# Token stages: the second copies of q's high part for head group 0 issued by ACT instead of SP

## The chip, the cores and the metric

The kernel runs on one core of one Trainium2 chip. The metric is the device time of the whole program in microseconds (us); lower is better. The engines are named as in the profile: PE is TensorE's matmuls and PEld its weight loads, DVE is VectorE, ACT is ScalarE, POOL is GpSimd, SP is SyncE, whose work here is to issue DMAs. An engine's name with a q behind it (SPq, ACTq) stands for what its sequencer does itself: DMA issues, semaphore waits, register work.

## What is computed

A transformer stack of two layers on 8192 tokens of width 512. The part that matters here is the cross attention that stands in both layers, ahead of a mixture of experts in the first layer and a light and heavy feed-forward in the second:

```python
q = split_heads(layernorm(x) @ Wq.T + bq)            # 16 heads of 32
k, v = split_heads(ctx @ Wk.T + bk), split_heads(ctx @ Wv.T + bv)   # 154 keys
scores = (q @ k.T) * tau + delta                      # then over sqrt(32)
x = x + softmax(scores) @ v  (heads joined) @ Wo.T + bo
```

## The kernel before, in words

`token_phase` is called once for each layer (l = 0 and l = 1). Its 8192 tokens are 16 groups of 512, and one turn of its loop works on one group; beside it, in the same turn, stand the end of the group before and the start of the group after. A turn has 16 steps (`st`), each a unit of 128 tokens and 4 heads; steps 0 to 3 are head group 0, steps 4 to 7 head group 1, and so on. The names in a turn i: `cur` is the group whose scores are computed, `nxt` the one after it, `prev` and `prev2` those before. The order of instructions on every engine is written out by hand, and engines meet through semaphores only. SP, POOL, DVE and PE run 12 of the turns in a hardware loop; ACT is unrolled.

The products of q and k are computed to full precision in one matmul per head: the rows of the moving side `kst` are k's high part, k's high part again and k's low part (32 rows each, then two rows for delta), and the stationary side `stack` holds under them q's high part, q's low part and q's high part again, and ones. So each head of q's high part is copied into `stack` twice, at rows 0 and 64, and its low part once, at row 32. These are copies from SBUF to SBUF between partitions, and they go by DMA: for each head group 4 heads, thus 8 copies of q's high part (L344) and 4 of its low part (L348), 64 KB each. SP issues all of them, in `stack_up`.

The chain for head group 0 of the next group of tokens, whose q is made ahead of its turn: PE's `query` (steps 10 and 11, L785) gives it, ACT adds the bias (`query_out`, L612, step 12), DVE rounds it to q's high part (`query_high`, L69, step 12), POOL subtracts to get q's low part (`query_low`, L407, step 12), SP copies both into `stack`, and PE's `scores` at step 0 of the next turn (L722) waits until `stacked0` has counted all 12 copies:

```python
if t == 0:
    pe.wait_ge(s[f"kv_in{g}"], 48 * i + 48)
    pe.wait_ge(s[f"stacked{g}"], STACK * i + STACK)
```

In each step ACT computes four exponentials (L691, each with a read of its sum behind it), which wait for DVE's `negmax` (L471) of the same unit. In layer 1, ACT also scales the finished tokens in steps 12 to 14 (`scaled`, L654). DVE copies transposed probabilities (L494) and normalises the finished group (L460) in steps 0 and 1. POOL scales the probabilities (L414). On SP, what follows `stack_up(i + 1, 0)` in a turn is, in layer 1, the store of z (L375, which waits for ACT's last `scaled`), then the store of xs (L378, which waits for DVE's `residual` of step 14), and the load of `xbo` (L381), each 1 MB.

Of the kernel before, what the change touches and what calls it, by code (L numbers as in the profile page):

```python
# [12 lines left out]
F32 = mybir.dt.float32  # L13
# [12 lines left out]
HEADS, DK = 16, 32  # L26
HG = P // DK
GROUPS = HEADS // HG
TROWS = HG * KTAIL
DC = D // P  # L30
# [208 lines left out]
def reached(engine, sem, value):  # L239

    if not (isinstance(value, int) and value <= 0):
        engine.wait_ge(sem, value)


def token_phase(nc, l, a, scr, c, x_in, x_rows):
    gate = l == 0
    with ExitStack() as ctx:
        def sb(name, shape, dt=F32):
            return ctx.enter_context(nc.sbuf_tensor(f"t{l}_{name}", shape, dt))
# [8 lines left out]
        qhigh, qlow = (sb(f"q_{part}", [P, 2, D], F32R) for part in ("high", "low"))  # L258
        qT = sb("qT", [P, 2, D])
        stack = sb("stack", [KROWS, HEADS, D], F32R)  # L260
# [13 lines left out]
        else:  # L274
# [4 lines left out]
        s = Sems(nc, ctx, f"t{l}",  # L279
                 "w_in wq_in kv_in0 kv_in1 kv_in2 kv_in3 x_in xbo_in ready ones x_stored z_stored "  # L280
                 "stacked0 stacked1 stacked2 stacked3 x_stats x_mv x_ve x_rstd xn xbo xnT_mm xnT_dve xnT_act "
                 "q_mm q_out q_high q_low scored negmax exped inv normed p_mm pTm pTt pv oT_out proj resid "
                 "s_stats s_mv s_ve s_rstd xl z z_mm zT_dve zT_act side_mm side_out top "
                 "ssq ssq_c rn score dot part_mm part logit")
# [39 lines left out]
        @block.sync  # L324
        def _(sp):
            sp.dma_start(x[:], rows(x_in, 0)).then_inc(s["x_in"], 16)
            sp.dma_start(wq[:], a[f"WqT{l}"].rearrange("(k p) n -> p k n", p=P)).then_inc(s["wq_in"], 16)
            with nc.allow_non_contiguous_dma(reason="biases by partition"):
                sp.dma_start(bq[:], a[f"bq{l}"].rearrange("(k p) -> p k", p=P)).then_inc(s["w_in"], 16)
            sp.dma_start(bo[:], a[f"bo{l}"].partition_broadcast(P)).then_inc(s["w_in"], 16)  # L330
            for g in range(GROUPS):
                load_kv(sp, 0, g)
            sp.dma_start(wo[:], a[f"WoT{l}"].rearrange("(k p) n -> p k n", p=P)).then_inc(s["w_in"], 16)
            if gate:
                sp.dma_start(wg[:], a["gateT"].rearrange("(k p) n -> p k n", p=P)).then_inc(s["w_in"], 16)
            else:
                sp.dma_start(rt[:], a["routing"].partition_broadcast(P)).then_inc(s["w_in"], 16)

            def stack_up(j, n):

                sp.wait_ge(s["q_high"], DC * j + n + 1)
                for at in (0, 2 * DK):
                    for h in range(HG):
                        sp.dma_start(stack[at:at + DK, HG * n + h, :].bitcast(F32),  # L344
                                     qhigh[h * DK:(h + 1) * DK, n % 2, :].bitcast(F32)).then_inc(s[f"stacked{n}"], 16)
                sp.wait_ge(s["q_low"], DC * j + n + 1)
                for h in range(HG):
                    sp.dma_start(stack[DK:2 * DK, HG * n + h, :].bitcast(F32),  # L348
                                 qlow[h * DK:(h + 1) * DK, n % 2, :].bitcast(F32)).then_inc(s[f"stacked{n}"], 16)

            def turn(i, par, prev2, prev, cur, nxt, nxt2):
                if cur:
                    stack_up(i, 1)
                if prev2 and gate:
                    sp.wait_ge(s["z"], TG * (i - 1))
                    sp.dma_start(rows(scr["xw"], i - 2, D), z[:]).then_inc(s["z_stored"], 16)
                if cur:
                    stack_up(i, 2)
                if prev and cur:
                    load_kv(sp, i, 2, GROUPS * i - 1)  # L360
                    load_kv(sp, i, 3, GROUPS * i)
                if nxt2:
                    reached(sp, s["xn"], TG * (i + 2))
                    sp.dma_start(x[:], rows(x_in, i + 2)).then_inc(s["x_in"], 16)
                if cur:
                    stack_up(i, 3)
                if cur and nxt:
                    load_kv(sp, i + 1, 0, GROUPS * i + 1)
                    load_kv(sp, i + 1, 1, GROUPS * i + 2)
                if nxt:  # L370
                    stack_up(i + 1, 0)
                if prev2 and not gate:
                    sp.wait_ge(s["z"], TG * (i - 1))
                    sp.wait_ge(s["score"], i - 1)
                    sp.dma_start(rows(scr["xs"], i - 2), z[:]).then_inc(s["z_stored"], 16)  # L375
                if prev:
                    sp.wait_ge(s["resid"], TG * i)
                    sp.dma_start(rows(x_rows, i - 1), xs[:]).then_inc(s["x_stored"], 16)  # L378
                if cur:
                    reached(sp, s["resid"], TG * i)  # L380
                    sp.dma_start(xbo[:], rows(x_in, i)).then_inc(s["xbo_in"], 16)  # L381

            turns(sp, turn)
            sp.wait_ge(s["z_stored"], 16 * NG)
            sp.wait_ge(s["x_stored"], 16 * NG)
# [220 lines left out]
        def _(act):  # L606
# [30 lines left out]
            def part_out(j):  # L637
                act.wait_ge(s["part_mm"], j + 1)
                reached(act, s["side_mm"], j)
                act.copy(part[:], ps[:, B_BANK, :]).then_inc(s["part"], 1)  # L640

            def square(j, t):
                act.wait_ge(s["xl"], TG * j + t + 1)
                if t == 0:
                    reached(act, s["rn"], j)
                else:
                    act.wait_ge(s["ssq"], TG * j + t)
                act.activation(junk2[:], z[:, t, 0:D], ACT.Square,
                               accum_out=ssq[:, t:t + 1]).then_inc(s["ssq"], 1)

            def scaled(j, tiles):
                act.wait_ge(s["rn"], j + 1)
                for t in tiles:
                    act.mul(z[:, t, 0:D], z[:, t, 0:D], rn[:, t:t + 1]).then_inc(s["z"], 1)  # L654

            def turn(i, par, prev2, prev, cur, nxt, nxt2):
                j = i - 2
                for st in range(UNITS):
                    if cur and st == 2:
                        query_out(i, 2)  # L660
                    if st == 2 and prev:
                        o_out(i - 1, 1 - par, 2)
                        p_tail_out(i - 1, GROUPS - 1)
                    if st in (6, 10, 14) and cur:
                        p_tail_out(i, st // TG - 1)
                    if cur and st == 4:
                        query_out(i, 3)
                    if st == 4 and prev:
                        o_out(i - 1, 1 - par, 3)
                    if st in (8, 12) and cur:  # L670
                        o_out(i, par, st // TG - 2)
                    if nxt and st == 12:
                        if not cur:
                            act.wait_ge(s["w_in"], W_IN)
                        query_out(i + 1, 0)
                    if cur and st == 0:
                        query_out(i, 1)
                    if gate and prev2 and st in (4, 12):
                        z_turned(j, Z_AT[st])
                    if nxt and st in (8, 10):  # L680
                        x_turned(i + 1, X_AT[st])
                    if not gate and prev2 and st in (3, 5, 7, 9):
                        square(j, (st - 3) // 2)
                    if cur:
                        u = st
                        act.wait_ge(s["negmax"], UNITS * i + u + 1)

                        reached(act, s["p_mm"], UNITS * i + u - 3)
                        for h in range(HG):
                            at = (h % 2) * KEYS  # L690
                            op = act.activation(pr[:, u % 4, :, h], ps[:, 2 * (u % 2) + h // 2, at:at + KEYS], ACT.Exp,  # L691
                                                bias=negmax[:, u, h:h + 1], accum_out=total[:, u, h:h + 1])
                        op.then_inc(s["exped"], 1)
                    if gate and prev2 and st == 13:
                        part_out(j)
                    if not gate and prev2 and st in (12, 13, 14):
                        if st == 12:
                            act.wait_ge(s["dot"], TG * (i - 1))
                        scaled(j, {12: (0,), 13: (1, 2), 14: (3,)}[st])

            unrolled(turn)

# [1324 lines left out]
```

## Time and profile before

| | |
|---|---|
| median of 3 runs | 4095.25 us (4093.11 to 4096.59) |
| the profiled execution | 4095.83 us, its span 4093.3 us |
| PE busy over the span | 3568.4 us, 87% |
| DVE, POOL, ACT busy | 67%, 47%, 36% |
| mean granted TensorE clock | 0.929 of full speed |
| L344, copies of q's high part | 1024 issues of 64 KB by SP |
| L348, copies of q's low part | 512 issues of 64 KB by SP |

The time stands 2.5 us above the span in the profiled execution; a change of the span is taken as the same change of the time. DMA issues are not counted as busy time. Times of rows are microseconds from the start of the span.

### The profile page before, as it was taken

To read this page: it belongs to the slowest core of one execution; us is meant where nothing else is said; L and a number is where in the kernel's file an instruction comes from. 1 tells how busy PE (TensorE), PEld (TensorE's weight loads), DVE (VectorE), ACT (ScalarE), POOL (GpSimd) and SP (SyncE) were. 2 spreads that over 40 slices of the span, in tenths; PEclk is the share of its full clock that TensorE was granted. 3 is DMA by queue.
4 is the path that set the end of the run, shared out by engine and by line. 5 is a ranking of instruction groups with operands and counts; after the bars stand their busy time and mean duration, and the time that the engine had idled before them with its cause. 6 is when DMAs were issued, how large, how long until landed. Compare 5 with 4: busy or idle time off the path is not lost. (4 is left out here: it accounts for less than half of the span.)

```text
span 4093.3 us, 56822 instructions
## 1 busy us (share of the span) xinstructions
PE 3568.4 (87%) x16277; PEld 2413.9 (59%) x16277; DVE 2724.6 (67%) x5471; ACT 1492.1 (36%) x5333; POOL 1918.5 (47%) x1784
## 2 busy tenths in 40 slices
PE   8599999999837999999996999999999696249998
PEld 4355555555426777777774555555555475227776
DVE  3477777777687677677673677777776443366665
ACT  0365666666400111111111666666666221201110
POOL 0255555555401777767773556555555232012332
PEclk9799999999955999999997999999999898569999
DMA  5455545454312666666664456555653555000111
GB/s 159 129 147 151 144 141 166 143 143 138 110 42 69 169 165 161 163 170 159 161 168 105 126 137 169 147 152 138 166 153 113 188 216 208 12 21 6 20 21 18
DMA packets 323211, 523.11 MB, mean 128 GB/s; under 512 B 59257, under 2 KB 104121, under 8 KB 322553
## 3 DMA queue, kind: packets, MB, share of 16 engines
q1 hardware_dynamic: 290808, 443.79, 36.6%
q0 software_dynamic: 32256, 77.65, 10.1%
q8 instruction: 58, 0.95, 0.1%
q14 instruction: 89, 0.72, 0.1%
HBM read 283.64 MB, written 136.96 MB: 103 GB/s over the span
## 5 line engine op out<-in xcount | busy, mean ns | idle before, releaser
L691 ACT ACTIVATE t_pr<-ps,t_negmax 128x154 f32<-128x154 f32 x2048 | 867.9, 547 | 529.4 <-DVE t_negmax L471 528.7
L414 POOL TENSOR_TENSOR t_pr<-t_pr,t_inv 128x616 f32<-128x616 f32 x512 | 642.6, 1256 | 616.3 <-DVE t_inv L486 613.6
L494 DVE COPY t_pTm<-ps 128x512 f32<-128x512 f32 x512 | 349.9, 683 | 315.0 <-PE ps L735 310.7
L785 PE MATMUL ps<-t_xnT,t_wq 128*128 128x512 f32 x1024 | 505.2, 617 | 19.1 <-ACT t_qT L612 18.9
L806 PE MATMUL ps<-t_wo,t_oT 128*128 128x512 f32 x1024 | 497.9, 610 | 7.8 <-DVE t_xs L503 6.6
L734 PEld LDWEIGHTS ps<-ident,t_pr 128*128 128x128 f32 x2048 | 317.9, 204 | 296.1 <-issue 258.0
L691 ACT ACTIVATION_READ_ACCUMULATOR t_pr<-ps,t_negmax 128x1 f32 x2048 | 472.1, 230 | 0.0
L471 DVE TENSOR_REDUCE t_negmax<-ps 128x4 f32<-128x616 f32 x512 | 403.1, 787 | 30.1 <-PE ps L722 29.6
L734 PE MATMUL ps<-ident,t_pr 128*128 128x128 f32 x2048 | 334.4, 286 | 51.7 <-DVE t_pTm L494 36.1
L722 PE MATMUL ps<-t_kst,t_stack 98*128 98x154 f32 x2048 | 340.1, 289 | 15.0 <-DMA t_stack<-t_q_low 13.2
L785 PEld LDWEIGHTS ps<-t_xnT,t_wq 128*128 128x128 f32 x1024 | 176.9, 192 | 229.4 <-issue 203.2
L74 PE MATMUL ps<-e_xT_high,e_wgu_high 128*128 128x512 f32 x768 | 307.2, 400 | 1.6 <-DVE e_xT_low L1248 1.6
L76 PE MATMUL ps<-e_xT_high,e_wgu_low 128*128 128x512 f32 x768 | 305.2, 397 | 0.0
L75 PE MATMUL ps<-e_xT_low,e_wgu_high 128*128 128x512 f32 x768 | 303.3, 395 | 0.0
L806 PEld LDWEIGHTS ps<-t_wo,t_oT 128*128 128x128 f32 x1024 | 176.0, 191 | 185.9 <-issue 166.4
L722 PEld LDWEIGHTS ps<-t_kst,t_stack 98*128 98x128 f32 x2048 | 272.7, 194 | 21.8 <-issue 19.5
L1208 POOL DMA_INDIRECT x_dram<-e_y,e_put_idx x128 | 246.1, 1923 | 30.8 <-issue 30.5
L407 POOL TENSOR_TENSOR t_q_low<-t_qT,t_q_high 128x512 fp32r<-128x512 f32 x128 | 174.0, 1359 | 167.9 <-DVE t_q_high L69 167.9
L1316 ACT ACTIVATE e_sig<-ps 128x512 f32<-128x512 f32 x96 | 57.5, 599 | 527.1 <-PE ps L76 527.1
L1288 DVE TENSOR_TENSOR e_h<-e_sig,ps 128x512 f32<-128x512 f32 x96 | 65.7, 685 | 245.9 <-ACT e_sig L1316 245.8
L1798 POOL TENSOR_TENSOR h_w_low<-c_hw,h_w_high 128x512 fp32r<-128x512 f32 x64 | 89.7, 1404 | 248.0 <-DVE h_w_high L69 248.0
L439 POOL TENSOR_TENSOR t_xbo<-t_xbo,t_bo 128x512 f32<-128x512 f32 x128 | 166.7, 1304 | 64.7 <-DMA t_xbo<-x_dram 64.0
(291 smaller groups left out, 7342.8 us busy)
## 6 DMA issues: line engine op xcount, KB each, us to landing
t_stack<-t_q_high SPq DMA_DIRECT2D x1024, 64.0 KB, 2.2
e_wgu_in<-in_gate_upT SPq DMA_DIRECT2D x32, 1536.0 KB, 6.5
t_stack<-t_q_low SPq DMA_DIRECT2D x512, 64.0 KB, 2.0
x_dram<-t_xs SPq DMA_DIRECT2D x32, 1024.0 KB, 5.7
t_kst<-kst_dram SPq DMA_DIRECT2D x128, 235.8 KB
e_wd_in<-in_downT SPq DMA_DIRECT2D x32, 768.0 KB
xs_dram<-t_z SPq DMA_DIRECT2D x16, 1032.0 KB
l_z<-xs_dram SPq DMA_DIRECT2D x16, 1032.0 KB
```

Source lines behind the costliest of these rows:

```text
L74: pe.matmul(out, left[0], right[0], start=start, stop=False)
L75: pe.matmul(out, left[0], right[1], start=False, stop=False)
L76: return pe.matmul(out, left[1], right[0], start=False, stop=stop)
L414: pool.tensor_tensor(p, p, inv[:, v, :].unsqueeze(1).to_broadcast([P, KEYS, HG]), ALU.mult).then_inc(s["normed"], 1)
L471: dve.tensor_reduce(negmax[:, u, :].rearrange("p (b h) -> p b h", b=2), ps[:, q:q + 2, 0:2 * KEYS].rearrange("p b (h n) -> p b h n", h=2), ...
L494: dve.tensor_copy(pTm[:, g % 2, :, t * P:(t + 1) * P], ps[:, 4, :].rearrange("p (h n) -> p h n", h=HG)).then_inc(s["pTm"], 1)
L691: op = act.activation(pr[:, u % 4, :, h], ps[:, 2 * (u % 2) + h // 2, at:at + KEYS], ACT.Exp, bias=negmax[:, u, h:h + 1], accum_out=total[ ...
L722: mm = pe.matmul(ps[:, 2 * (u % 2) + h // 2, at:at + KEYS], stack[:, HG * g + h, t * P:(t + 1) * P], kst[:, g, h * KEYS:(h + 1) * KEYS], s ...
L734: pe.transpose(ps[:, 4, h * P:(h + 1) * P], pr[:, v % 4, 0:P, h], ident[:])
L785: mm = pe.matmul(ps[:, A_BANK, :], wq[:, k, n * P:(n + 1) * P], xnT[:, k, :], start=(k == 0), stop=(k == DC - 1))
L806: mm = pe.matmul(ps[:, A_BANK, :], oT[:, par, k, t * P:(t + 1) * P], wo[:, k, :], start=(k == 0), stop=(k == DC - 1))
L1208: pool.indirect_dma_start(out=scr["x1"][:, :], out_offset=bass.IndirectOffsetOnAxis(ap=put_idx[:, n:n + 1], axis=0), in_=y[q][:, n, :], in ...
```

## The change

For head group 0 alone, SP no longer issues the four second copies of q's high part (to rows 64 to 95 of `stack`). ACT issues them, behind its exponentials of step 14 (in layer 1 behind `scaled` of that step too), after a wait for `q_high`. The count that PE waits for is the same 12 copies. Head groups 1 to 3 are left as they were.

```diff
             def stack_up(j, n):
 
                 sp.wait_ge(s["q_high"], DC * j + n + 1)
-                for at in (0, 2 * DK):
+                for at in (0, 2 * DK) if n else (0,):
                     for h in range(HG):
                         sp.dma_start(stack[at:at + DK, HG * n + h, :].bitcast(F32),
                                      qhigh[h * DK:(h + 1) * DK, n % 2, :].bitcast(F32)).then_inc(s[f"stacked{n}"], 16)
...
+            def stack_again(j):
+                act.wait_ge(s["q_high"], DC * j + 1)
+                for h in range(HG):
+                    act.dma_start(stack[2 * DK:3 * DK, h, :].bitcast(F32),
+                                  qhigh[h * DK:(h + 1) * DK, 0, :].bitcast(F32)).then_inc(s["stacked0"], 16)
+
...
                         scaled(j, {12: (0,), 13: (1, 2), 14: (3,)}[st])
+                    if nxt and st == 14:
+                        stack_again(i + 1)
```

On ACT, before, in steps 13 to 15 of a turn of layer 1 and the first of the next (the exponentials are L691, `scaled` is L654, `query_out` L612):

```order
L654 ACTIVATE t_z<-t_z,t_rn 128x512 x2
L624 COPY t_pTt<-ps 104x512
L691 ACTIVATE t_pr,t_total<-ps,t_negmax 128x154 x4
L654 ACTIVATE t_z<-t_z,t_rn 128x512
L691 ACTIVATE t_pr,t_total<-ps,t_negmax 128x154 x4
L612 ACTIVATE t_qT<-ps,t_bq 128x512
L691 ACTIVATE t_pr,t_total<-ps,t_negmax 128x154 x8
```

The same place in the change, where the lines behind the insertion have other numbers:

```order
L660 ACTIVATE t_z<-t_z,t_rn 128x512 x2
L624 COPY t_pTt<-ps 104x512
L697 ACTIVATE t_pr,t_total<-ps,t_negmax 128x154 x4
L660 ACTIVATE t_z<-t_z,t_rn 128x512
L645 DMA t_stack<-t_q_high 32x512 x4
L697 ACTIVATE t_pr,t_total<-ps,t_negmax 128x154 x4
L612 ACTIVATE t_qT<-ps,t_bq 128x512
```

Four DMA issues now stand between the exponentials of step 14 and those of step 15; in layer 0 they stand there too, with no `scaled` ahead of them. On SP, at the end of a turn of layer 0:

```order
 L322 DMA t_vt<-vt_dram 104x128
-L344 DMA t_stack<-t_q_high 32x512 x8
+L344 DMA t_stack<-t_q_high 32x512 x4
 L348 DMA t_stack<-t_q_low 32x512 x4
 L378 DMA x_dram<-t_xs 128x4x512
```

Four issues are gone ahead of the copies of q's low part and of what is queued behind them. This is so in each of the 16 turns of a layer that make a next q: once before the first scores, and 15 times between two turns.

## Rows read from the trace of the kernel before

**Rows 1.** Windows of both layers: length; busy PE, PEld, DVE, ACT, POOL; clock, DMA share.

```profile
320.00:1035.00 715.00, 704.08 (x3527) 418.82 (x3526) 536.71 (x1141) 434.95 (x1751) 393.30 (x340) 1.00 0.52 148
2460.00:3090.00 630.00, 601.71 (x2867) 348.95 (x2866) 484.46 (x1035) 422.76 (x1676) 372.93 (x316) 0.99 0.56 151
```

**Rows 2.** Timeline of PE at the end of a turn of layer 0: start, us, what.

```profile
562.26 0.65 PE L722 MATMUL ps<-t_kst,t_stack 98*128 98x154 f32 x4
563.50 1.98 PE L785 MATMUL ps<-t_xnT,t_wq 128*128 128x512 f32 x4 [0.59 <-ACT t_qT L612]
```

**Rows 3.** Timeline of SP at the same place.

```profile
551.41 4.95 SPq L344 DMA_DIRECT2D t_stack<-t_q_high  x8
556.40 2.49 SPq L348 DMA_DIRECT2D t_stack<-t_q_low  x4
559.09 0.43 SPq L378 DMA_DIRECT2D x_dram<-t_xs  x1
559.72 0.41 SPq L381 DMA_DIRECT2D t_xbo<-in_x  x1
```

**Rows 4.** Timeline of ACT at the same place, first exponential of units and query_out.

```profile
558.09 0.55 ACT L691 ACTIVATE t_pr<-ps,t_negmax 128x154 f32<-128x154 f32 x1 [0.86 <-DVE t_negmax L471]
...
559.24 0.54 ACT L691 ACTIVATE t_pr<-ps,t_negmax 128x154 f32<-128x154 f32 x1
...
561.23 0.54 ACT L691 ACTIVATE t_pr<-ps,t_negmax 128x154 f32<-128x154 f32 x1 [1.45 <-DVE t_negmax L471]
```

**Rows 5.** Semaphore waits of ACT's own sequencer, windows 557.5:559 and 2749.9:2750.3.

```profile
L242 ACTq EVENT_SEMAPHORE  x1: 17/17/17, 558.1 to 558.1; - x1
L242 ACTq EVENT_SEMAPHORE  x1: 17/17/17, 2750.1 to 2750.1; - x1
```

**Rows 6.** Timeline of layer 1 at the end of a turn: PE, ACT and SP.

```profile
2754.11 0.65 PE L722 MATMUL ps<-t_kst,t_stack 98*128 98x154 f32 x4
2750.51 0.59 ACT L691 ACTIVATE t_pr<-ps,t_negmax 128x154 f32<-128x154 f32 x1
2752.01 0.78 ACT L654 ACTIVATE t_z<-t_z,t_rn 128x512 f32<-128x512 f32 x1
2753.08 0.54 ACT L691 ACTIVATE t_pr<-ps,t_negmax 128x154 f32<-128x154 f32 x1 [0.28 <-DVE t_negmax L471]
2749.92 2.49 SPq L348 DMA_DIRECT2D t_stack<-t_q_low  x4
2752.99 0.43 SPq L375 DMA_DIRECT2D xs_dram<-t_z  x1
```

**Rows 7.** L348 and L344 by source in 551:559 and 526:533: issue ns, landing.

```profile
L348 SPq DMA_DIRECT2D t_stack<-t_q_low x4: 590/590/591, 556.4 to 558.3; - x4
DMA to landing us min/median/max: 2.0/2.0/2.2
L344 SPq DMA_DIRECT2D t_stack<-t_q_high x8: 527/590/1532, 526.9 to 532.3; - x8
DMA to landing us min/median/max: 3.1/3.9/5.8
```

**Rows 8.** Gathers on POOL's queue behind a 768 KB load of SP's, 1530:1536.

```profile
L1194 POOL DMA_INDIRECT e_xe<-xw_dram,e_idx x4: 946/955/1037, 1531.2 to 1535.0; - x4
DMA to landing us min/median/max: 3.4/4.1/4.8
```

**Rows 9.** Timeline of DVE at the end of the turn of rows 2.

```profile
556.06 0.69 DVE L503 TENSOR_TENSOR t_xs<-ps,t_xbo 128x512 f32<-128x512 f32 x1 [1.84 <-PE ps L806]
...
563.26 0.78 DVE L471 TENSOR_REDUCE t_negmax<-ps 128x4 f32<-128x616 f32 x1
```

**Rows 10.** Timeline of PE where scores of step 0 waited for copies.

```profile
158.83 1.11 PE L722 MATMUL ps<-t_kst,t_stack 98*128 98x154 f32 x4 [5.85 <-DMA t_stack<-t_q_low]
210.51 0.65 PE L722 MATMUL ps<-t_kst,t_stack 98*128 98x154 f32 x4 [1.20 <-issue]
266.74 0.67 PE L722 MATMUL ps<-t_kst,t_stack 98*128 98x154 f32 x4 [0.59 <-DMA t_stack<-t_q_low]
```

## The prediction

> **What bounds the kernel now.** The windows come first: in layer 0 from 320 to 1035 us, PE is busy for 704.08 of 715 us at full clock, and in layer 1 for 601.71 of 630 us [rows 1]. PE is the bound of the token stages, so a change counts only if it moves PE. Then the timelines of the five engines at one turn boundary of each layer. In layer 0 the scores of step 0 start at 562.26, directly behind PE's own work, with no idle time shown ahead of them [rows 2]; SP's last copy of q's low part is issued by 558.89 (556.40 + 2.49) [rows 3], and such a copy lands 2.0 to 2.2 us after its issue begins [rows 7]. The last of the four begins at 558.3, so everything is there by 560.5, 1.8 us before PE wants it. In layer 1 the scores start at 2754.11; the last low copy begins at 2749.92 + 3 x 0.62 = 2751.78 and lands at 2753.8 to 2754.0, 0.1 to 0.3 us ahead [rows 6, 7]. So before the change the copies are just in time, and SP's issue time is the price of PE only where a row says so: before the first scores (5.85 us of waiting at 158.83 in layer 0, and one like it in layer 1) and at three of the 30 boundaries: 1.20 us, 0.59 us and, of the same kind as the latter, 0.94 us in layer 1 [rows 10].
>
> **What the change takes from SP.** Four issues of 0.62 us each, 2.5 us (4.95 us for eight [rows 3]), leave SP ahead of q's low copies. At an ordinary boundary nobody waits for SP there, so this is worth nothing on PE. Ahead of the first scores of each layer the whole chain waits for SP: 2.5 us each, 5.0 us together. At the three boundaries of [rows 10] at most the idle time shown: 1.2 + 0.6 + 0.9 us; I take 2.5 us, since at the first of them ACT's `query_out` is the next limit. Gain: 7.5 us.
>
> **What the change gives to ACT.** The disputed point is when ACT issues. Counted naively, the four issues start when the exponentials of step 14 are through. The rows say otherwise. Each unit of exponentials has a semaphore wait of the sequencer's own ahead of it (for PE's transposes). The one that belongs to step 15 is executed at 558.1, as the first exponential of step 14 starts (558.09), and not after its last (559.24) [rows 4, 5]. So ACT's sequencer walks past instructions whose waits are met while the engine still works them off; a DMA issue is sequencer work and stands in just this place of the order. In layer 1 the wait of step 15 is executed at 2750.1, before even the first exponential of step 14 starts (2750.51) and though `scaled` (2752.01) lies between [rows 5, 6]. I therefore let the four issues begin at 558.12 in layer 0 and 2750.1 in layer 1, at SP's pitch of 0.62 us, for which ACT has no row of its own.
>
> In layer 0 they end at 560.6. Step 15's exponentials start at 561.23, when DVE's maximum is there [rows 4]: 0.6 us of cover, ACT loses nothing. If the pitch were 0.76 us (eight issues behind a load begin from 526.9 to 532.3, one of them lasting 1532 ns [rows 7]) they would end at 561.2, still free. In layer 1 they end at 2752.6 against 2753.08 [rows 6]: 0.5 us of cover, and 0.1 us lost at the longer pitch. Behind ACT's issues are queued those exponentials and then `query_out` of step 0, for which PE already waits 0.59 us in layer 0 [rows 2]; that is who pays if the cover is gone.
>
> **When the last copy lands.** Layer 1: the last issue begins at 2751.96. SP stores z only at 2752.99, so nothing large is in flight, and the landing is 2.0 to 2.2 us: 2754.0 to 2754.2 against 2754.11. I take +0.05 us for each of the 12 ordinary boundaries, 0.6 us.
>
> Layer 0: the last issue begins at 558.12 + 1.86 = 559.98. But SP, with 2.5 us less to do, has its 1 MB store and 1 MB load out sooner: its low copies end at 556.4, the store waits for DVE's residual, done at 556.75 [rows 9], and goes out about 557, the load about 557.6, instead of 559.09 and 559.72 [rows 3]. ACT's copies, which used to be ahead of these two on SP's queue, now meet them on the DMA engines. The price has no row of its own. From below: 2.0 us, as with idle engines. From above: 5.8 us, the slowest copy issued right behind a 1 MB load on the same queue (the fastest of these took 3.1) [rows 7]. Nearest is a small transfer on another queue beside SP's load: POOL's gathers, where the one with most of the load in flight lands after 4.8 us and the one with least after 3.4 [rows 8]. That is up to 1.4 us for company. I take 1.1 us, a landing of 3.1 us, thus 563.1: the scores of step 0 are 0.85 us late.
>
> The Trainium skill has a rule for this in "DMA: Bandwidth & Descriptors", section "Queues, rings and completion order": a DMA engine takes turns between queues, but a whole packet of one queue at a time. By it a copy on ACT's own queue waits for a packet or so of SP's load and not for all of it, and the 5.8 us of the same queue would be too dear; no run here has shown it yet.
>
> What 0.85 us costs PE: DVE's maximum of step 0 starts at 563.26 with no idle time ahead of it, so DVE is busy until then [rows 9], while the scores are through by 562.91. So 0.35 us of it is hidden on DVE, and of what is left the chain maximum, exponentials, `query_out` of the next step goes on with it. I take 0.4 us at each of 13 ordinary boundaries of layer 0: 5.2 us.
>
> **Sum.** 5.2 + 0.6 - 7.5 = -1.7 us on a profiled time of 4095.83 us, which is 0.6 us above the median of the runs shown. Forecast: 4095 us, no change to speak of. A measurement of this kernel tells about 0.2% (8.2 us) from nothing.
>
> **The rivals.**
>
> *ACT issues late (slower).* The sequencer may not begin a DMA before the engine has worked off what stands ahead. Then the issues run from 559.6 to 562.1 in layer 0 (559.24 + 0.38 of pitch), and step 15's exponentials, `query_out` and PE's L785 are 0.9 us late; the last copy lands at 561.5 + 3.1 = 564.6, 2.3 us late, less 0.35. In layer 1 they run from about 2752.7 to 2755.2, and the last copy lands beside the store of z at 2754.5 + 3.1 = 2757.6, 3.5 us late, of which about 2.8 reach PE. 13 x 1.95 + 12 x 2.8 - 5 = 54: 4150 us. For it: no row shows a DMA issue on ACT. Against it: [rows 5]. It decides from the point where the issues begin after about 558.4.
>
> *The sequencer's lead is shorter (slower, little).* The row at 2750.1 has nine or more instructions not yet done ahead of it. If the DMAs get less of a lead than that wait did, by 0.4 to 0.8 us, layer 1 loses 12 x 0.6 = 7 us: 4102 us.
> The Trainium skill's "Advanced Engine Details and Errata", section "Engine Queue Depths", gives ScalarE a queue of 8, which would set the issues back to where some of the exponentials have run; the row at 2750.1 does not bear this out for a semaphore wait.
>
> *Company on the DMA engines is dear (slower).* If the last copy in layer 0 lands like the copies behind a load on the same queue, after 3.9 to 5.8 us [rows 7], the scores are 1.65 to 3.5 us late, 1.3 to 3.2 after DVE's cover: 13 x that is 17 to 41 us, thus 4106 to 4130 us. For it: both large transfers are out before ACT's first issue. Against it: the queues are two.
>
> *SP's relief is worth all it can be (faster).* No contention, the whole 8 us at the first scores and the three boundaries, and 0.1 to 0.2 us more at each ordinary boundary of layer 1, where the low copies were only just ahead: 4095.8 - 7.7 - 2 = 4086 us. It needs ACT's copies to land in 2.0 us in layer 1 and under 2.6 in layer 0. The same rival stops at -5 or less if two engines that issue at once share what issues, which the first scores would show.
>
> **How the numbers follow.** Forecast 0.50; ACT late 0.10; shorter lead 0.08; dear company 0.20; full relief 0.12. The forecast's own range is 4088 to 4103. The range must leave out no more than 2 in 10: below, 4086, the bound of the full relief; above, 4128, which takes in nearly all of the dear company and leaves out the late ACT. Faster than -0.2% is the full relief: 0.12. Slower by over 0.2% is the late ACT, the dear company and a part of the shorter lead: 0.33. The rest, 0.55, is no change.
>
> **What the profile after would show.** Right: ACTq's four issues begin within 0.1 us of the first exponential of step 14, about 0.6 us apart; step 15's exponentials still wait for DVE; SP's store and load of layer 0 come 2 us sooner; the wait of PE's L722 for a DMA shrinks at the first scores from 5.85 to 3.4 us, and new waits of under 1 us for copies of q's high part appear at the boundaries of layer 0 and none to speak of in layer 1. Wrong: issues after the last exponential, waits of PE above 1.5 us at each boundary, or ACT's issues much longer than 0.6 us.

## The result, and the profile after

| | before | after |
|---|---|---|
| median | 4095.92 us (4093.11 to 4099.02, 4 runs) | 4205.4 us (4202.37 to 4212.62, 4 runs) |
| span of the profiled execution | 4093.3 us | 4210.9 us |
| mean granted TensorE clock | 0.929 | 0.915 |
| PE busy | 3568.4 us | 3613.6 us |

The ratio is 1.027 [1.0252, 1.0287]: the change costs 109 us. The forecast was 4095 us in a range of 4086 to 4128, so the prediction was wrong, and the range too.

Where PE lost the time stands in its costliest groups. On the page of the kernel after, the scores have 96.4 us of idle time ahead of them, 74.3 of it ended by DMAs of q's high part (the same group of before, on its line L722, had 15.0 us of it and was 340.1 us busy, 289 ns a matmul; the query's group had a mean of 617 ns):

```profile
PE 3613.6 (86%) x16277; PEld 2438.6 (58%) x16277; DVE 2731.5 (65%) x5471; ACT 1494.1 (35%) x5333; POOL 1919.8 (46%) x1784
L793 PE MATMUL ps<-t_xnT,t_wq 128*128 128x512 f32 x1024 | 533.5, 647 | 10.5 <-ACT t_qT L612 10.5
L730 PE MATMUL ps<-t_kst,t_stack 98*128 98x154 f32 x2048 | 350.5, 296 | 96.4 <-DMA t_stack<-t_q_high 74.3
```

Waiting grew by 96.4 - 15.0 = 81.4 us and PE's busy time by 45.2 us, together 126.6 us; against it stand shorter waits for other engines (8.6 us of them the query's wait for ACT, 10.5 for 19.1), and the span grew by 117.6 us. By stages, counted from PE's first matmuls in each, the token stage of layer 0 grew by 101.2 us (1037.8 to 1139.0) and that of layer 1 by 14.4 us (992.4 to 1006.8). The 3.5 us in what follows layer 1's token stage (882.2 to 885.7) are not of this change: that part takes 884 to 887 us in the traces of all seven experiments below too. Two things are therefore to be explained: the waits, and why the same matmuls took longer (the query's 647 ns for 617).

The view of waits of PE by releaser, three rows for layer 0 (150 to 1160 us) and then two for layer 1 (2280 to 3300 us); columns are the total, how many, and the longest:

```profile
PE ps L730 <- DMA t_stack<-t_q_high: 64.4, 12, 6.1
PE ps L730 <- issue: 12.4, 3, 5.8
PE ps L730 <- DMA t_stack<-t_q_low: 3.3, 1, 3.3
...
PE ps L730 <- DMA t_stack<-t_q_high: 9.9, 2, 6.1
PE ps L730 <- DMA t_stack<-t_q_low: 3.3, 1, 3.3
```

In layer 0 the scores of step 0 wait at every boundary, 2.2 us at the first and 4.2 to 6.1 us at the others. The three waits put down to "issue" are at the same place of a turn. In layer 1 it is three boundaries of 15 (the two above and one of 3.1 us put down to "issue"); elsewhere nothing. The timeline of PE gives the same in order (start, us, what, and in brackets the idle time before it). Of the 13 scores of step 0 between 320 and 1140 us, the first, one in the middle with the row behind it, and the last:

```profile
338.96 1.13 PE L730 MATMUL ps<-t_kst,t_stack 98*128 98x154 f32 x4 [5.88 <-DMA t_stack<-t_q_high]
...
603.33 1.13 PE L730 MATMUL ps<-t_kst,t_stack 98*128 98x154 f32 x4 [6.05 <-DMA t_stack<-t_q_high]
604.26 3.70 PE L793 MATMUL ps<-t_xnT,t_wq 128*128 128x512 f32 x4
...
1134.69 1.11 PE L730 MATMUL ps<-t_kst,t_stack 98*128 98x154 f32 x4 [5.80 <-issue]
```

Twelve turns take 1134.69 - 338.96 = 795.7 us, 66.3 us each. In the kernel before, the same twelve take 1035.69 - 325.37 = 710.3 us, 59.2 us each:

```profile
325.37 0.65 PE L722 MATMUL ps<-t_kst,t_stack 98*128 98x154 f32 x4
...
1035.69 0.65 PE L722 MATMUL ps<-t_kst,t_stack 98*128 98x154 f32 x4
```

So a boundary of layer 0 costs 7.1 us. From the first scores to those of the last of the 15 boundaries the kernel before needs 876.9 us and this one 979.9 us, 103 us more, nearly the whole result. Not all of the 7.1 us is the wait. The first query matmuls behind the wait take 3.70 us, where those of [rows 2] take 1.98, and the scores themselves 1.13 instead of 0.65. The windows around this boundary say why (length; busy PE, PEld, DVE, ACT, POOL; clock, DMA share):

```profile
596.50:603.30 6.80, 0.78 (x6) 0.49 (x4) 1.57 (x9) 2.00 (x9) 0.85 (x1) 0.91 0.65 189
603.30:607.50 4.20, 4.17 (x8) 2.26 (x9) 3.00 (x5) 1.70 (x8) 2.03 (x2) 0.50 0.06 16
608.50:609.00 0.50, 0.50 (x5) 0.50 (x4) 0.00 (x0) 0.00 (x0) 0.00 (x0) 0.56 0.41 98
609.00:609.50 0.50, 0.50 (x6) 0.50 (x5) 0.43 (x1) 0.00 (x0) 0.00 (x0) 1.00 0.28 70
```

After PE has stood idle for some 6 us, the granted clock is 0.50 (1.2 GHz) until about 608.9, 5.6 us, and then full again. That work would take 2.8 us at full clock. Windows of a quarter of a microsecond behind each of the 15 waits of layer 0 show between 3.3 and 6.6 us at half clock, which costs 1.7 to 3.3 us, 38 us together and 2.5 us in the mean. On the other side PE's wait of 0.59 us for `query_out` [rows 2], which stood at 13 boundaries of layer 0, is gone.

Now the sources of the wait, at the same boundary. SP first, from its copies of q's low part on:

```profile
588.66 2.49 SPq L348 DMA_DIRECT2D t_stack<-t_q_low  x4
591.72 0.43 SPq L378 DMA_DIRECT2D x_dram<-t_xs  x1
592.35 0.41 SPq L381 DMA_DIRECT2D t_xbo<-in_x  x1
```

Then ACT, the exponentials of steps 14 and 15 and its own sequencer's issues among them:

```profile
592.87 0.55 ACT L697 ACTIVATE t_pr<-ps,t_negmax 128x154 f32<-128x154 f32 x1 [0.87 <-DVE t_negmax L471]
592.90 0.52 ACTq L645 DMA_DIRECT2D t_stack<-t_q_high  x1
...
593.45 1.32 ACTq L645 DMA_DIRECT2D t_stack<-t_q_high  x1
...
594.79 1.39 ACTq L645 DMA_DIRECT2D t_stack<-t_q_high  x2
596.29 0.56 ACT L697 ACTIVATE t_pr<-ps,t_negmax 128x154 f32<-128x154 f32 x1 [1.72 <-DVE t_negmax L471]
```

ACT did as forecast: the issues begin 0.03 us after the first exponential of step 14 starts, and the exponentials of step 15 still wait for DVE, as in [rows 4]. ACT's busy time is the same to 2 us, and it is not ACT that is late. But SP's store and load stand ahead of ACT's first issue, by 1.18 and 0.55 us, where before they were issued behind all twelve copies [rows 3]. By source, ACT's copies of this boundary and those of 320 to 1140 us (issue in ns as min/median/max, and from the start of the issue to the landing):

```profile
L645 ACTq DMA_DIRECT2D t_stack<-t_q_high x4: 515/680/1316, 592.9 to 595.6; - x4
DMA to landing us min/median/max: 7.6/7.8/8.2
L645 ACTq DMA_DIRECT2D t_stack<-t_q_high x52: 514/639/1337, 328.7 to 1127.1; - x52
DMA to landing us min/median/max: 5.9/7.5/8.2
```

The last copy begins at 595.6 and cannot be there before 595.6 + 7.6 = 603.2; PE starts at 603.33. What held it is in the DMA queues, for which the windows 592.5 to 598.5, 598.5 to 601.5 and 601.5 to 603.3 us stand here one after the other (packets, MB, share of the 16 engines; q1 is SP's queue, q10 is ACT's):

```profile
q1 hardware_dynamic: 787, 1.58, 93.5%
...
q1 hardware_dynamic: 258, 0.51, 60.7%
q10 hardware_dynamic: 141, 0.20, 29.3%
...
q10 hardware_dynamic: 51, 0.07, 11.0%
q1 hardware_dynamic: 11, 0.01, 2.1%
```

Not a packet of ACT's queue is carried from 592.90 to 598.5, while 1.58 MB of SP's queue are, its store and half of its load; the copies come in as the load runs out. The two large transfers are 2.1 MB, and 787 + 258 + 11 packets of q1 are just these 2.1 MB.

In layer 1 a boundary without this company looks like this in the source view, 2862 to 2872 us, and the scores start at 2869.15 with no wait, since SP issues its stores only from 2868.03 on:

```profile
L645 ACTq DMA_DIRECT2D t_stack<-t_q_high x4: 514/610/613, 2865.1 to 2867.0; - x4
DMA to landing us min/median/max: 2.0/2.0/2.1
```

### The profile page after: what moved, and what is told of

The parts are those of the page before. It is cut to its first block and busy times, and to the rows that moved or that the text cites. A ratio compares the mean times of both kernels' runs of the same rounds, so it can differ in the third digit from the quotient of the medians.

```text
span 4210.9 us, 56822 instructions
## 1 busy us (share of the span) xinstructions
PE 3613.6 (86%) x16277; PEld 2438.6 (58%) x16277; DVE 2731.5 (65%) x5471; ACT 1494.1 (35%) x5333; POOL 1919.8 (46%) x1784
## 5 line engine op out<-in xcount | busy, mean ns | idle before, releaser
L793 PE MATMUL ps<-t_xnT,t_wq 128*128 128x512 f32 x1024 | 533.5, 647 | 10.5 <-ACT t_qT L612 10.5
L730 PE MATMUL ps<-t_kst,t_stack 98*128 98x154 f32 x2048 | 350.5, 296 | 96.4 <-DMA t_stack<-t_q_high 74.3
L742 PE MATMUL ps<-ident,t_pr 128*128 128x128 f32 x2048 | 340.1, 290 | 51.4 <-DVE t_pTm L494 36.6
L730 PEld LDWEIGHTS ps<-t_kst,t_stack 98*128 98x128 f32 x2048 | 282.2, 200 | 105.6 <-issue 105.4
L793 PEld LDWEIGHTS ps<-t_xnT,t_wq 128*128 128x128 f32 x1024 | 186.3, 202 | 227.1 <-issue 212.8
L439 POOL TENSOR_TENSOR t_xbo<-t_xbo,t_bo 128x512 f32<-128x512 f32 x128 | 166.6, 1303 | 59.2 <-DMA t_xbo<-x_dram 58.6
```

The source lines that it names most:

```text
L730: mm = pe.matmul(ps[:, 2 * (u % 2) + h // 2, at:at + KEYS], stack[:, HG * g + h, t * P:(t + 1) * P], kst[:, g, h * KEYS:(h + 1) * KEYS], s ...
L742: pe.transpose(ps[:, 4, h * P:(h + 1) * P], pr[:, v % 4, 0:P, h], ident[:])
L793: mm = pe.matmul(ps[:, A_BANK, :], wq[:, k, n * P:(n + 1) * P], xnT[:, k, :], start=(k == 0), stop=(k == DC - 1))
```

## The experiments

The theory after this reading: ACT's copies are late because SP, relieved of four issues, has its 1 MB store and 1 MB load out ahead of them, and a copy behind them lands only when they have drained, on whichever queue it is. Rivals: copies issued by ACT are slow in themselves, or beside SP's issues; the loss comes from ACT's engine being held up; one of the two transfers alone does it; a queue of its own shelters ACT's copies at least in part. The kernel before, beside which these ran, took 4096.2 us (27 runs) with the first four and 4094.52 us (15 runs) with the last three.

### The store and the load behind the copies

SP waits until all twelve copies have landed before it issues either of the two. ACT still issues the four copies in step 14.

```diff
+                if cur and nxt:
+                    sp.wait_ge(s["stacked0"], STACK * (i + 2))
                 if prev:
                     sp.wait_ge(s["resid"], TG * i)
                     sp.dma_start(rows(x_rows, i - 1), xs[:]).then_inc(s["x_stored"], 16)
```

> The changed kernel, but SP waits until all 12 copies of head group 0 have landed before it issues the store of xs and the load of xbo. Theory (collision): ACT's copies were late by 5 to 6 us in layer 0 because SP's 1 MB store and 1 MB load, issued earlier than before, stood ahead of them on the DMA engines. Then the copies land in 2.0 to 2.2 us again, PE waits for none of them at the ordinary boundaries of layer 0, and the time is 4080 to 4100 us. Rival (ACT's queue): a copy issued by ACT is slow by itself, or is issued too late; then the waits of 5 to 6 us stay, and so does 4190 to 4215 us.

Measured: 4090.85 us (10 runs), ratio 0.9982 [0.9972, 0.9991]; clock 0.929. The whole loss is gone, as the theory had it (4080 to 4100 us). ACT's copies in layer 0, by source:

```profile
L647 ACTq DMA_DIRECT2D t_stack<-t_q_high x50: 514/612/613, 319.7 to 1030.7; - x50
DMA to landing us min/median/max: 2.0/2.0/2.1
```

Issued by ACT at the same place, behind the same exponentials, the copies land in 2.0 us, and PE's waits for them are gone from the view of waits. So neither ACT's issuing nor its place in ACT's program costs anything here; the order against SP's two transfers does. PE's busy time is back at 3569.0 us and the clock at 0.929, so the 45 us of longer matmuls belonged to the waits.

### Only the load behind the copies

The same wait, but behind the store: the store goes out ahead of ACT's copies, the load after them.

```diff
                     sp.dma_start(rows(x_rows, i - 1), xs[:]).then_inc(s["x_stored"], 16)
+                if cur and nxt:
+                    sp.wait_ge(s["stacked0"], STACK * (i + 2))
                 if cur:
```

> The changed kernel, but only the load of xbo waits for the 12 copies; the store of xs goes out ahead of ACT's copies as in the change. Theory (collision): the lateness is the bytes that stand ahead. With 1 MB in place of 2 MB the last copy lands after 4.5 to 5.5 us, the scores of step 0 are 2 to 3 us late at each of about 13 boundaries of layer 0, and the time is 4115 to 4150 us. Rival (only the load from HBM holds copies back, the store does not): as in the run where both wait, 4080 to 4100 us. Rival (any transfer ahead costs the same): 4190 us or more.

Measured: 4097.5 us (10 runs), ratio 1.0005 [0.9996, 1.0015], no difference from the kernel before that can be told, but 6.7 us more than with both transfers behind the copies. The store alone costs much less than I had expected (4115 to 4150 us); the time lies in the range of the rival by which only the load holds copies back. The copies and PE's wait for them (150 to 1180 us):

```profile
L647 ACTq DMA_DIRECT2D t_stack<-t_q_high x52: 514/615/1375, 320.0 to 1034.3; - x52
DMA to landing us min/median/max: 2.0/2.5/3.6
PE ps L732 <- DMA t_stack<-t_q_high: 5.5, 12, 2.2
```

A landing of 2.5 us instead of 2.0, a wait of 0.5 us a boundary. The long issue of 1.3 to 1.4 us, one in four, is still there; it goes with the store in these runs, since it is missing where the load alone is ahead (below).

### ACT's issues two steps earlier

```diff
-                    if nxt and st == 14:
+                    if nxt and st == 12:
                         stack_again(i + 1)
```

> The changed kernel, but ACT issues the four copies behind its exponentials of step 12 instead of step 14, about 6.7 us earlier, and so ahead of SP's store and load. Theory (collision): they land before the large transfers start, no boundary of layer 0 waits, and what SP saves stays: 4080 to 4090 us. ACT's exponentials of step 13 start 0.3 us behind the last issue at the earliest, so up to 0.5 us more at each of 30 boundaries if SP's and ACT's issues slow each other: then 4085 to 4100 us. Rival (ACT's queue is slow by itself): about 8 us of landing would now be hidden too, since the scores come 10 us after the issues, so this run does not speak against it; it tells whether SP and ACT can issue at the same time (both pitches stay 0.62 us) or not (1.2 us).

Measured: 4093.5 us (11 runs), ratio 0.9994 [0.9985, 1.0003], no difference that can be told, and outside the 4080 to 4090 us of the theory. It fits the second range, 4085 to 4100, but not by the condition that stood with it, that SP's and ACT's issues slow each other. In layer 0:

```profile
L645 ACTq DMA_DIRECT2D t_stack<-t_q_high x48: 521/622/866, 370.7 to 1024.1; - x48
DMA to landing us min/median/max: 2.0/2.1/2.4
```

The copies are now issued while SP issues its own eight, and the issue of one takes 622 ns against 612 where ACT issues alone, and one of SP's copies of q's high part 590 ns against 591 in the kernel before (medians): two engines that issue at once do not slow each other. The copies are out before SP's store and load, so the loss is gone without a wait of SP for them. What is gained at the first scores is partly lost in layer 1, where PE waits for ACT's copy of the transposed probabilities 8.7 us in 14 waits (2.9 us in two before). I read this as the four issues standing ahead of that copy on ACT; it was not tried by itself.

### SP issues the same four copies, behind its store and load

ACT issues nothing. This separates the order from the queue.

```diff
-                for at in (0, 2 * DK):
+                for at in (0, 2 * DK) if n else (0,):
...
                     sp.dma_start(xbo[:], rows(x_in, i)).then_inc(s["xbo_in"], 16)
+                if nxt:
+                    for h in range(HG):
+                        sp.dma_start(stack[2 * DK:3 * DK, h, :].bitcast(F32),
+                                     qhigh[h * DK:(h + 1) * DK, 0, :].bitcast(F32)).then_inc(s["stacked0"], 16)
```

> The kernel before, with ACT issuing nothing: SP issues the four second copies of head group 0 last in its turn, behind its store of xs and load of xbo. Theory (collision): the copies stand behind 2 MB again, now on the same queue, and land 5 to 8 us late in layer 0; in layer 1, where the load is issued at the boundary itself, they are later still. 4200 to 4290 us. Rival (what is slow is ACT's queue, or the change of queues): SP's last issue in layer 0 begins near 560 us of the old timeline and would land by 562.2, no wait in layer 0, and layer 1 pays about 3 us at 13 boundaries: 4130 to 4145 us.

Measured: 4396.65 us (4 runs), ratio 1.0727 [1.0711, 1.0744], above the range I had given. By source, layer 0 (320 to 1140 us) and layer 1 (2460 to 3300 us), each with its landings:

```profile
L384 SPq DMA_DIRECT2D t_stack<-t_q_high x52: 591/756/1462, 335.0 to 1136.1; - x52
DMA to landing us min/median/max: 5.8/7.5/8.5
L384 SPq DMA_DIRECT2D t_stack<-t_q_high x48: 590/958/1387, 2459.5 to 3249.7; - x48
DMA to landing us min/median/max: 7.0/8.4/10.0
```

The first pair is the point: on the same queue as the store and the load the copies land after 5.8, 7.5 and 8.5 us (least, median, most), on ACT's own queue after 5.9, 7.5 and 8.2. The queue of its own is worth nothing here, and the loss in layer 0 is nearly the same: its token stage takes 1147.6 us against 1139.0 in the change and 1037.8 before. The time is higher here because layer 1 pays too: SP issues the copies behind the stores of z and xs and the load, which wait for ACT's last `scaled`, and PE waits there 151.4 us in 13 waits, up to 13.1 us each.

### Only the store behind the copies

The load first, then the wait, then the store.

```diff
-                if prev:
-                    sp.wait_ge(s["resid"], TG * i)
-                    sp.dma_start(rows(x_rows, i - 1), xs[:]).then_inc(s["x_stored"], 16)
                 if cur:
                     reached(sp, s["resid"], TG * i)
                     sp.dma_start(xbo[:], rows(x_in, i)).then_inc(s["xbo_in"], 16)
+                if cur and nxt:
+                    sp.wait_ge(s["stacked0"], STACK * (i + 2))
+                if prev:
+                    sp.wait_ge(s["resid"], TG * i)
+                    sp.dma_start(rows(x_rows, i - 1), xs[:]).then_inc(s["x_stored"], 16)
```

> The changed kernel, but SP issues the load of xbo first, then waits for the 12 copies of head group 0, then issues the store of xs: now the load alone stands ahead of ACT's copies, where the run before had the store alone (4097.5 us, copies land after 2.5 us in the median of layer 0). Theory (backlog: what counts is how much is still to be moved when the copies are issued, whatever it is): 1 MB ahead is nearly gone by the time of the last copy, landing 2.5 to 4 us, 4090 to 4115 us. Rival (loads from HBM are what holds copies back): the landing stays at 6 to 8 us and the time at 4170 us or more.

Measured: 4128.38 us (4 runs), ratio 1.0082 [1.0066, 1.0097]. It lies between the two expectations: the load alone costs more than the theory had, and less than the rival by which loads are what holds copies back. The copies in layer 0, and PE's waits for them:

```profile
L647 ACTq DMA_DIRECT2D t_stack<-t_q_high x52: 514/610/618, 326.9 to 1065.0; - x52
DMA to landing us min/median/max: 3.5/4.5/5.4
PE ps L732 <- DMA t_stack<-t_q_high: 24.2, 12, 4.0
```

In the median a load of 1 MB ahead holds the copies by 2.5 us, a store of 1 MB by 0.5. One boundary of each kernel shows where that comes from. With the load ahead (issued at 386.61, ACT's first copy at 387.60), q1's share of the DMA engines in 391.0 to 391.5 and 391.5 to 392.0 us:

```profile
q1 hardware_dynamic: 91, 0.17, 89.0%
q10 hardware_dynamic: 22, 0.04, 19.4%
...
q10 hardware_dynamic: 71, 0.10, 89.1%
q1 hardware_dynamic: 31, 0.05, 26.3%
```

With the store ahead (issued at 378.09, ACT's first copy at 379.25), 381.0 to 381.5 and 381.5 to 382.0 us:

```profile
q1 hardware_dynamic: 91, 0.19, 101.2%
...
q1 hardware_dynamic: 86, 0.16, 93.6%
q10 hardware_dynamic: 8, 0.02, 10.8%
```

The store has drained 3.9 us after its issue, the load 5.4 us after its own, and ACT's queue starts in earnest where q1 ends, both times. Counted from ACT's first issue that is 2.7 against 4.4 us. The 1.7 us between them is most of the 2.0 between the two medians of the landing. Why the bytes of a load move later than those of a store I have not tried to find out.

### Half of the load ahead

The store and the first half of the load go out ahead of ACT's copies, the second half behind the wait (POOL waits for both halves).

```diff
-                    sp.dma_start(xbo[:], rows(x_in, i)).then_inc(s["xbo_in"], 16)
+                    sp.dma_start(xbo[:, 0:2, :], rows(x_in, i)[:, 0:2, :]).then_inc(s["xbo_in"], 16)
+                if cur and nxt:
+                    sp.wait_ge(s["stacked0"], STACK * (i + 2))
+                if cur:
+                    sp.dma_start(xbo[:, 2:4, :], rows(x_in, i)[:, 2:4, :]).then_inc(s["xbo_in"], 16)
```

> The changed kernel, with the load of xbo in two halves: the store and the first half (1.5 MB together) are issued ahead of ACT's copies as in the change, the second half waits for the copies. Theory (backlog): between 1 MB (wait of 0.5 us) and 2 MB (wait of 5.4 us) ahead, thus 2 to 3.5 us at each boundary of layer 0, landing 4 to 6 us, and 4125 to 4155 us. Rival (a threshold, such as a queue that is full with 2 MB and not with less): landing near 2.5 us and 4100 us at most.

Measured: 4147.52 us (4 runs), ratio 1.0128 [1.0111, 1.0145], within the 4125 to 4155 us of the theory. The landings in layer 0:

```profile
L649 ACTq DMA_DIRECT2D t_stack<-t_q_high x52: 514/622/1351, 323.0 to 1077.0; - x52
DMA to landing us min/median/max: 4.1/5.3/6.4
```

No threshold shows: each further piece ahead costs more. It is not the bytes alone, since 1 MB of load costs more than 1 MB of store. The five kernels in a row (the kernel before took 4096.2 us beside the first two, 4094.52 beside the next two and 4095.92 beside the last):

| ahead of ACT's copies in layer 0 | median landing | time |
|---|---|---|
| nothing | 2.0 us | 4090.85 us |
| store (1 MB) | 2.5 us | 4097.5 us |
| load (1 MB) | 4.5 us | 4128.38 us |
| store and half of the load (1.5 MB) | 5.3 us | 4147.52 us |
| store and load (2 MB) | 7.5 us | 4205.4 us |

### The relief alone

The kernel before, but ahead of the first scores of each layer ACT issues the second copies. No boundary between two turns is touched.

```diff
-                for at in (0, 2 * DK):
+                first = isinstance(j, int) and j == 0
+                for at in (0,) if n == 0 and first else (0, 2 * DK):
...
+                    if i == -1 and st == 14:
+                        stack_again(i + 1)
```

> The kernel before, but ahead of the first scores of each layer, where the chain waits for SP and nothing large is on the DMA engines, ACT issues the four second copies; at all 30 boundaries SP issues all 12 as before. If the gain of the change lies there alone: the first scores of each layer come 4.1 us sooner, as they did in the change (154.75 against 158.83), and the time is 8 us under the kernel before: 4085 to 4091 us. If the gain of the run with the wait was elsewhere: 4096 us.

Measured: 4090.68 us (11 runs), ratio 0.9989 [0.998, 0.9998], in the expected range but at its upper end: 3.8 us under the kernel before, where 8 were expected. PE's wait for copies at the first scores is 3.3 us instead of 5.85 [rows 10], and they start at 156.19 instead of 158.83. That is 2.6 us sooner in layer 0 and not the 4.1 that I took over from the trace of the change; 1.1 of those 4.1 us are there before any copy is waited for (PE's first matmuls of the stage at 135.37 instead of 136.48). The traces with such a gain have first scores from 154.56 to 156.19, and the start of the stage lies between 135.1 and 136.5 in all nine traces, whichever kernel it is. The first experiment gives SP's relief at all 16 places of a layer and has 0.9982; the two intervals overlap, so nearly all that the change had to give lies at the first scores, and the ordinary boundaries add nothing that can be told. No version measured is faster than these two.

## Why the prediction was wrong

*What bounds the kernel; copies just in time.* Right. PE is the bound, and the 1.8 us that layer 0 had in hand [rows 2, 3] were the whole of its margin.

*What the change takes from SP.* Right at the first scores. They wait 3.3 us instead of 5.85, the 2.5 us forecast. Counted from PE's first matmuls of the stage they come 3.0 us sooner in layer 0 (19.4 us instead of 22.4) and 2.2 us in layer 1 (20.1 instead of 22.3), 5.2 us together against 5.0. The kernel with this relief alone is 3.8 us faster than before (4090.68 against 4094.52), and the 5.0 us lie within its interval. Where SP's transfers are held back, 5.35 us of the whole 7.5 came (4090.85 against 4096.2), and 7.5 lies within that interval too.

*When ACT issues.* Right, at 0.03 us behind the first exponential against the 0.03 that [rows 4, 5] gave, and ACT loses nothing. In layer 1 the first issue (2865.13) begins 0.41 us before the first exponential of step 14 (2865.54), as the wait did in [rows 5, 6]. The rival in which ACT issues late is out, and so is the one with the shorter lead.

The queue depth of 8 that the Trainium skill gives for ScalarE ("Advanced Engine Details and Errata", "Engine Queue Depths") did not set the issues back: the trace has the first at 2865.13, with four exponentials, the four reads behind them and `scaled`, nine instructions, still to start.

*The pitch of ACT's issues.* 0.61 us where no store is in flight, as taken. With the store ahead one of the four lasts 1.3 to 1.4 us (also in the experiment with the store alone, and not in the one with the load alone), so the last issue begins 2.7 us after the first instead of 1.86. How much of this reaches the landing is not shown: the copies wait for SP's bytes in any case.

*The landing in layer 1.* Right for 12 boundaries: 2.0 to 2.1 us, no wait. Missed: at three of the 15, the large transfers do meet the copies (waits of 3.1, 6.1 and 3.7 us). At the first two boundaries there is no store of z to hold SP back: at the first the load alone goes out (2384.39, beside ACT's first copy at 2384.30), at the second the store (2445.87) is ahead of all four and the load (2446.50) ahead of three. At the third (scores at 2694.36) the order is the usual one, but ACT's last issue, begun at 2688.19, lasts 1.69 us instead of 0.61, SP's store of z goes out at 2689.23 before it ends, and this copy lands after 6.1 us; why that issue was long no run shows. I had read one boundary from the middle of the layer and multiplied it.

*The landing in layer 0.* **This is the step that failed.** The prediction has SP's store and load out ahead of ACT's copies, which is what happened, and prices the company at "a landing of 3.1 us", "from above: 5.8 us". Measured: 5.9 to 8.2 us, 7.5 as the median. So even the upper bound was below all 52 that were measured there. Two things were wrong in how it was bounded. First, [rows 7] are copies behind one transfer of 1 MB (and six smaller loads of keys and values), and here two of 1 MB went ahead: with one of them the landings are 2.5 or 4.5 us, with both 7.5. I had the 2 MB in the text and took the bound of one. Second, I leaned to the low end because "the queues are two", and took a gather in company [rows 8] for the nearest case. The four copies on SP's queue land as late as on ACT's.

The rule of the Trainium skill that the forecast weighed ("DMA: Bandwidth & Descriptors", "Queues, rings and completion order": turns between the queues, a packet at a time) would have made the copies' wait a packet or so. The trace does not agree: 1.58 MB of q1 go by before the first packet of q10. It does not show where ACT's copies stood in that time, at the DMA engines behind SP's or not yet there. Whether the bytes of the two queues take turns on any single DMA engine later, from 598.5 on, it doesn't tell either, since it doesn't name the engine of a packet.

*What the lateness costs PE.* I took half of it to be hidden on DVE. The wait of PE is all there (4.2 to 6.1 us, 5.3 as the mean of the 13 between 320 and 1140 us), and DVE hid none of it: its maximum behind the scores of 603.33 starts at 604.50 after 6.39 us without work. What it does repay is PE's wait of 0.59 us for `query_out`, which is gone. The wait brings a second price that no term of the sum had: the clock at half behind it, 2.5 us in the mean. With the measured landing and the measured issues the step comes out right. In the terms of the forecast: the last issue at 558.12 + 2.7 = 560.8, landing 7.6 us later at 568.4, against 562.26: 6.2 us late, for a wait of 6.05 us at the boundary shown. With the mean wait a boundary comes to 5.3 + 2.5 - 0.6 = 7.2 us, against 7.1 measured.

*The sum.* The recorded sum gives 4094.1 us; the forecast put it at 4095. Put together from what was measured, and to that extent an estimate, layer 0 has 76.8 us of waits for copies and 38.0 for the half clock, less 1.8 us that PE waited there before, 7.7 of shorter waits for `query_out`, 3.0 at the first scores and 0.8 of half clock behind them: 101.5 us, against 101.2 of its stage. In the same way layer 1 has 13.0 and 7.9, less 1.2, 0.7, 2.2 and 0.8: 16 us, against 14.4. The half clock also accounts for the busy time: 45.8 us at the 18 boundaries, less 1.5 at the two first scores, against the 45.2 by which PE's busy time grew.

*The rivals.* "Company on the DMA engines is dear" was the mechanism, and its chance of 0.20 the second highest. Its price, 17 to 41 us, was at most two fifths of the 103 us measured in layer 0, for the same reason as the range.

*What stays open.* Why q10 gets nothing while q1's transfers are under way: that the order of arrival decides fits the change and all seven experiments, if an arrival is the end of an issue (the third boundary of layer 1), but no run here shows single DMA engines, and none tells a turn at the DMA engines from one at whatever hands the copies to them. And why the gathers of [rows 8] come through with at most 4.8 us: they start from another engine's queue, behind 768 KB, and were not tried with 2 MB ahead.

## What to carry to other kernels

When a queue of DMA issues is shortened, look at what stands behind the removed ones: a bulk transfer that was issued just after the urgent copies now goes out ahead of them, and what decided here was the bytes still to be moved ahead of the copies, a load's more than a store's, on whichever queue the copies were. Bound the price of such a meeting by all the bytes that are ahead, and add to a new wait of PE of some microseconds the stretch at half clock behind it (here 2.5 us). The remedy was one wait (bulk transfers behind the landed copies) or moving only the issues that somebody waits for; either kept the 4 to 5 us that the change had to give.

## What the runs showed of the hardware

- Two queues of two engines were no shelter: 64 KB copies behind 2 MB of another engine's queue landed after 5.9 to 8.2 us, on that same queue after 5.8 to 8.5.
- In the median a load of 1 MB from DRAM held copies issued 1 us later by 2.5 us, a store of 1 MB by 0.5.
- ACT's sequencer issues DMAs in 0.61 us each, beside its engine's activations and without delay to them, and at the same pace while SP issues too (0.62). With a store of 1 MB just ahead, one issue in four took 1.3 to 1.4 us.
- After waits of 3.1 to 6.1 us without matmuls the granted clock was 0.50 for 3.3 to 6.6 us, with PE busy (17 boundaries of the change).
